# State-space slots: the output projection multiplies as plain fp32, without high and low parts

## The reference, cut to what matters

```python
proj = xn @ in_proj_w.T
z, xc, B, C, dt = jnp.split(proj, [...], axis=-1)
...                                    # convolution, silu, scan over time -> ys
y = jnp.moveaxis(ys, 0, 1).reshape(b, s, D_INNER)
y = _rms(y, inner_norm_w)              # divides by one root mean square per token, times a weight
y = y * jax.nn.silu(z)
out = y @ out_proj_w.T                 # 3072 -> 256
return x + out * RES_MULT
```

## Time and profile before

| | us |
|---|---|
| time, median of 3 runs (3034.8 to 3040.43) | 3035.02 |
| span of the profiled execution | 3067.1 |
| of it, state-space stage, from about | 1517 |
| PE / DVE / ACT / POOL busy over the span | 2711.5 / 2384.6 / 2110.9 / 1973.4 |

### The profile page before, as it was taken

One profiled execution on the slowest core, in us unless ns is written; L12 is line 12 of the kernel. 1 busy time (PEld: TensorE's weight loads), 2 busy tenths in 40 slices (PEclk: granted clock), 3 DMA queues, 4 the chain that ended last, 5 costly groups with the idle time before them and its releaser, 6 DMA issues.

```text
span 3067.1 us, 58582 instructions
## 1 busy us (share of the span) xinstructions
PE 2711.5 (88%) x17318; PEld 2120.1 (69%) x17318; DVE 2384.6 (78%) x5972; ACT 2110.9 (69%) x4670; POOL 1973.4 (64%) x1697
## 2 busy tenths in 40 slices
PE   4799999998569888379799999999999999999997
PEld 2466666665469765267588788787887878878786
DVE  3466666666377589558599999998899999999896
ACT  4444454443255466346599999998999999999996
POOL 3322222214424214555399999998999999999998
PEclk7799999997889899689899999999999999999999
DMA  6355445455766544446777776767666666676673
GB/s 168 94 176 170 168 165 185 149 195 168 238 178 199 168 154 151 157 128 199 230 240 237 236 237 205 220 204 220 219 206 217 205 210 216 205 224 199 203 218 113
DMA packets 320436, 588.35 MB, mean 192 GB/s; under 512 B 47888, under 2 KB 138800, under 8 KB 319632
## 3 DMA queue, kind: packets, MB, share of 16 engines
q1 hardware_dynamic: 305776, 545.07, 57.6%
q0 software_dynamic: 14352, 39.54, 3.5%
HBM read 464.44 MB, written 124.17 MB: 192 GB/s over the span
## 4 chain that ended last, share of the span: by engine, by line
POOL 34%; issue 10%; ACT 3%; DVE 1%; PE 1%; DMA 1%; POOLq 1%; SPq 0%; ACTq 0%; DVEq 0%
POOL mm L2706 8%; POOL y L2719 7%; POOL yz L2723 7%; POOL y L2733 6%; POOL y_lo L2712 6%; ACT mt L2636 1%; DVE cv L2789 1%; DMA wi<-ssm_wi_split 1%; POOLq L2382 1%; ACT ys L2650 0%; ACT mt L2656 0%; DVE bank L2860 0%; ACT L2671 0%; POOL first L2748 0%; PE bank L64 0%
## 5 line engine op out<-in xcount | busy, mean ns | idle before, releaser
L2706 POOL TENSOR_TENSOR mm<-mt,cb 128x512 f32<-128x512 f32 x384 | 490.2, 1299 | 56.9 <-ACT mt L2656 54.9
L2636 ACT ACTIVATE mt<-a_wide,a_tok 128x128 f32<-128x128 f32 x1536 | 487.1, 389 | 3.5 <-POOL mm L2706 2.5
L2789 DVE SCALAR_TENSOR_TENSOR cv<-bank,taps,cv 128x509 f32<-128x509 f32 (+2 forms) x576 | 429.3, 745 | 13.6
L64 PE MATMUL bank<-f,wi 128*128 128x512 f32 x768 | 322.4, 420 | 14.7 <-DMA wi<-ssm_wi_split 14.6
L65 PE MATMUL bank<-f,wi 128*128 128x512 f32 x768 | 305.7, 398 | 0.0
L66 PE MATMUL bank<-f,wi 128*128 128x512 f32 x768 | 305.7, 398 | 0.0
L2723 POOL TENSOR_TENSOR yz<-y,zs 128x512 f32<-128x512 f32 x192 | 249.2, 1298 | 15.0
L2712 POOL TENSOR_TENSOR y_lo<-yz,y_hi 128x512 fp32r<-128x512 f32 x192 | 246.2, 1282 | 8.4 <-ACT y_hi L2661 6.5
L2719 POOL TENSOR_TENSOR y<-t 128x512 f32<-128x512 f32 x192 | 246.0, 1281 | 0.0
L2529 PE MATMUL bank<-mm,x_tok 128*64 128x128 f32 x3072 | 226.4, 283 | 13.1 <-POOL mm L2706 13.1
L2733 POOL TENSOR_TENSOR y<-y,ys 128x512 f32<-128x512 f32 x184 | 237.6, 1292 | 0.1
(11 more groups left out here) (476 smaller groups left out, 8067.5 us busy)
## 6 DMA issues: line engine op xcount, KB each, us to landing
wi<-ssm_wi_split SPq DMA_DIRECT2D x192, 512.0 KB
a_wide<-a_scratch SPq DMA_DIRECT2D x192, 512.0 KB
l_fw<-ffn_split SPq DMA_DIRECT2D x72, 768.0 KB
ea<-ea_scratch SPq DMA_DIRECT2D x384, 128.0 KB
wo<-ssm_wo_split SPq DMA_DIRECT2D x192, 256.0 KB, 4.1
sorted_scratch<-ex_zeros SPq DMA_DIRECT2D x96, 130.5 KB
ssm_wi_split<-l_s_out SPq DMA_DIRECT2D x24, 512.0 KB
ey_x<-sorted_scratch SPq DMA_DIRECT2D x94, 130.5 KB
```

Source lines behind the costliest of these rows:

```text
L64: pe.matmul(out, wh, xh, start=first, stop=False)
L2636: i = act.activation(mt[:, h, chunk(j)], a_wide[:, g % R, h, chunk(j)], ACT.Relu, bias=a_tok[:, s * NJ + j, 2 * t + h:2 * t + h + 1], scal ...
L2706: pl.tensor_tensor(mm[:, :, ts], mt[:, :, ts], cb[:, js, :].rearrange("p j t -> p (j t)") .unsqueeze(1).broadcast_to([P, 2, TS // 2]), ALU ...
L2789: dve.scalar_tensor_tensor(cv[:, a:TS], bank[:, X, 0:TS - a], taps[:, t, k:k + 1], cv[:, a:TS], ALU.mult, ALU.add).then_inc(ph["tap"], 1)
```

## The change

The out-projection weights are no longer split. In the first stage GpSimd computes the low half only for the 512 in_proj columns of a state-space tile, ScalarE makes its copy in two instructions (512 and 256 columns, the second as plain fp32), and the scratch for them holds 256 columns instead of 512. In `ssm`, `output_high` and `output_low` are gone, `project_out` reads `yz` and `wo` directly with one plain fp32 matmul per bank, and `yz` is released by `out` instead of `y_lo`.

```diff
@@ ScalarE, first stage
-                    if n >= NT:
-                        done(act, "s_wo", n - NT)
-                    act.activation(s_out[:, 0:MLP], s_raw[:, 0:MLP], ACT.Copy).then_inc(ph["high"], 1)
+                    if n < NT:
+                        act.activation(s_out[:, 0:MLP], s_raw[:, 0:MLP], ACT.Copy).then_inc(ph["high"], 1)
+                        return
+                    act.activation(s_out[:, 0:MP_IN], s_raw[:, 0:MP_IN], ACT.Copy)
+                    done(act, "s_wo", n - NT)
+                    act.activation(s_out[:, MP_IN:MLP].bitcast(F32), s_raw[:, MP_IN:MLP], ACT.Copy).then_inc(ph["high"], 1)
@@ GpSimd, first stage
-                    pl.tensor_tensor(s_out[:, MLP:2 * MLP], s_raw[:, 0:MLP], s_out[:, 0:MLP].bitcast(F32), ALU.subtract).then_inc(ph["low"], 1)
+                    w = MLP if n < NT else MP_IN
+                    pl.tensor_tensor(s_out[:, MLP:MLP + w], s_raw[:, 0:w], s_out[:, 0:w].bitcast(F32), ALU.subtract).then_inc(ph["low"], 1)
@@ ssm
-        wo = sb("wo", [P, R, 2 * MP_OUT], F32R)
+        wo = sb("wo", [P, R, MP_OUT])
-        y_hi, y_lo = sb("y_hi", [P, TS], F32R), sb("y_lo", [P, TS], F32R)
@@ TensorE, project_out
-                    done(pe, "y_lo", g)
+                    done(pe, "yz", g)
                     landed(pe, "wo", g)
                     if t == 0:
                         done(pe, "evac", s - 1)
                     for m in range(KD):
-                        a = m * P
-                        i = mm3(pe, bank[:, OUT + m, :], (wo[:, g % R, a:a + P], wo[:, g % R, MP_OUT + a:MP_OUT + a + P]),
-                                (y_hi[:], y_lo[:]), t == 0, t == LAST)
+                        i = pe.matmul(bank[:, OUT + m, :], wo[:, g % R, m * P:(m + 1) * P], yz[:, g % 2], start=t == 0, stop=t == LAST)
@@ ScalarE: output_high and its call in beat k (item k-4) are gone
-                    act.activation(y_hi[:], yz[:, g % 2], ACT.Copy).then_inc(ph["y_hi"], 1)
@@ GpSimd: output_low and its call in beat k (item k-4) are gone
-                    pl.tensor_tensor(y_lo[:], yz[:, g % 2], y_hi[:].bitcast(F32), ALU.subtract).then_inc(ph["y_lo"], 1)
@@ GpSimd, outputs
-                    done(pl, "y_lo", g - 2)
+                    done(pl, "out", g - 2)
                     pl.tensor_tensor(yz[:, g % 2], y[:], zs[:, g % NS], ALU.mult).then_inc(ph["yz"], 1)
```

More of the change, by code:

```diff
@@ L129, in program @@
         wi_dram = nc.dram_tensor("ssm_wi_split", (NCT, P, 2 * MP_IN), F32, kind="Internal").ap()
-        wo_dram = nc.dram_tensor("ssm_wo_split", (NCT, P, 2 * MP_OUT), F32, kind="Internal").ap()
+        wo_dram = nc.dram_tensor("ssm_wo_scaled", (NCT, P, MP_OUT), F32, kind="Internal").ap()
         a_drams = (a_dram, nc.dram_tensor("a_scratch1", (HM, T), F32, kind="Internal").ap())
@@ L428, in keep @@
                     else:
-                        parts = s_out[:].bitcast(F32).rearrange("p (h c) -> p h c", h=2)
-                        sp.dma_start(wi_dram[n - NT].rearrange("p (h c) -> p h c", h=2), parts[:, :, 0:MP_IN]).then_inc(ph["s_kept"], 16)
-                        sp.dma_start(wo_dram[n - NT].rearrange("p (h c) -> p h c", h=2), parts[:, :, MP_IN:MLP]).then_inc(ph["s_kept"], 16)
+                        parts = s_out[:].bitcast(F32)
+                        sp.dma_start(wi_dram[n - NT].rearrange("p (h c) -> p h c", h=2),
+                                     parts.rearrange("p (h c) -> p h c", h=2)[:, :, 0:MP_IN]).then_inc(ph["s_kept"], 16)
+                        sp.dma_start(wo_dram[n - NT], parts[:, MP_IN:MLP]).then_inc(ph["s_kept"], 16)
                 def clear(a):
@@ L2430, in weights_out @@
                     done(sp, "out", g - R)
-                    sp.dma_start(wo[:, g % R, :].bitcast(F32), wo_dram[g % NCT]).then_inc(ph[f"wo{g % R}"], 16)
+                    sp.dma_start(wo[:, g % R, :], wo_dram[g % NCT]).then_inc(ph[f"wo{g % R}"], 16)
                 def inputs(s):
@@ L2656, in decays @@
                         act.activation(mt[:, :, ts], mt[:, :, ts], ACT.Exp, scale=-1.0).then_inc(ph["ex"], 1)
-                def output_high(g):
-                    done(act, "yz", g)
-                    done(act, "out", g - 1)
-                    act.activation(y_hi[:], yz[:, g % 2], ACT.Copy).then_inc(ph["y_hi"], 1)
                 def tokens(g):
@@ L2680, in _ @@
                         convolve(k)
-                    if has(k - 4):
-                        output_high(k - 4)
                     if has(k):
@@ L2707, in decayed @@
                                          .unsqueeze(1).broadcast_to([P, 2, TS // 2]), ALU.mult).then_inc(ph["mm"], 1)
-                def output_low(g):
-                    done(pl, "y_hi", g)
-                    done(pl, "out", g - 1)
-                    pl.tensor_tensor(y_lo[:], yz[:, g % 2], y_hi[:].bitcast(F32), ALU.subtract).then_inc(ph["y_lo"], 1)
                 def outputs(g):
@@ L2765, in _ @@
                         decayed(k - 1)
-                    if has(k - 4):
-                        output_low(k - 4)
                     if has(k - 3):
```

## The result

The changed kernel takes 3054.59 us (median of 4 runs, 3054.1 to 3058.65), the kernel before 3036.2 in the same comparison. The ratio is 1.0061, 95% interval [1.0046, 1.0075]: **slower by 18.4 us, 0.6%**. The forecast was 3069, or +34, with a range of 3048 to 3090.

A forecast was written before the change was run, and what follows sets the result against it. The prediction took TensorE (PE) to bound the ordinary beat. Its terms, +8.2, +24.6, +4.1, -2.0 and -1, with 0 for the first stage, came to +34 us: 3035 + 34 = 3069, range 3048 to 3090.

The forecast's parts named there:

- That TensorE bounds the ordinary beat: State-space stage: TensorE's own work is 7.64 us a beat, becoming 7.96 (early beats 7.86, becoming 8.18); chance 0.72.
- what GpSimd gives back: Ordinary beats: removing `y_lo` (1.28 us) returns no more than GpSimd's lag behind TensorE, 0.03 to 0.16 us a beat.
- +0.32 a beat: Output projection on TensorE: six products (1.40 us) give way to four fp32 passes (1.72 us), taken as 0.316.
- The first load: Rival, output projection: the first weight load is exposed each time, +0.10 in 190 beats, +19 us, 3088; chance 0.13.
- Slots: State-space stage, 24 beats each: cost 7.6 us, give back 2.3 + 1.2, so +4.1 each; six make +24.6.
- the stall: One beat 5.7 us too long on a late weight DMA: TensorE arriving later may take up some, -1, up to -5.
- The end of the program: After the last beats: some 2.5 us won on GpSimd's chain, limited by the last projection at the lower clock, -2.0.
- The rule on the weight loads' share: Weight loads busy 82% would mean TensorE has 18% left and GpSimd, at 99%, is the bound.
- the first rival: Ordinary beats: GpSimd is the bound and TensorE has room, -0.65 x 168 = -109 us, 2926 or so; chance 0.07.
- Two of the signs: Changed profile: GpSimd busy about 83% and waiting for ScalarE's `mt`; the chain of waits moved from GpSimd to PE.
- the first stage: GpSimd's subtraction shrinks (15 us) without gain; 24 more small ScalarE instructions, some 5 us; counted 0, with -3 to +4.
- the slots' ends: Three beats there run 4.4 us over TensorE's own work, of which about 1.2 go; giving back more favours 3048.

The follow-up runs named there:

- TensorE's part alone: The kernel before with only TensorE's output product changed to one plain fp32 matmul per bank, weights' low part left out; `y_hi` and `y_lo` still made: 3073.99 us, ratio 1.0123.
- GpSimd's alone: The kernel before without GpSimd's `y_lo` subtraction, TensorE multiplying `y_hi` in its place, six products as before: 3015.96 us, ratio 0.9933.
- the runs with the copies alone: The kernel before with one edit, ScalarE copying a first-stage state-space tile in two instructions (512, then 256 columns after the scaling wait): 3026.74 us, ratio 0.9965.
- the run with one copy: The changed kernel with ScalarE's first-stage copy put back to one instruction of 768 columns after the scaling wait: 3066.75 us, ratio 1.0103.
- the version with two products: The kernel before with ScalarE's two copies and two products per bank, fp32r `yz` by the weights' high and low parts, y's low part dropped: 2977.51 us, ratio 0.9804.

## Why the prediction was right, and where it was off

- **That TensorE bounds the ordinary beat** and that what GpSimd gives back is at most 0.03 to 0.16 a beat, is shown from both sides. TensorE's part alone costs 37, GpSimd's alone gains 21, where its 246.2 us of busy time and the chain promised ten times that.
- **+0.32 a beat for four passes at 0.43 against six products at 0.233**: measured 1.72 for the four, and 7.95 where 7.96 was forecast (8.18 in the early beats, as forecast). The first load was not exposed in the ordinary beats: the record of the four is 1.88 long and not 1.98.
- **Slots**: the forecast was 194.2 between two `mean_square`, +4.1; 24 beats of the changed kernel take 194.2. The stage from first to last scores pass was forecast 36.9 longer, before the stall, and is 35.9 in the profiled pair.
- **The end of the program**: -2.0 forecast, -3.8 in the profiled pair (-0.5 in the run where `y_hi` and `y_lo` stayed). The beat with the late weight DMA gave nothing clear: the 24 beats around it went from 195.4 to 199.4, where the forecast had PE take up 1 us; in the other experiments with the plain product they took 196.1 to 200.2.
- **The rule on the weight loads' share**, which the prediction cites from the Trainium skill, would have led to the first rival. With PEld at 82% TensorE had no room, and GpSimd's removal alone gave 21 us, not 109. Here the measurement decides against reading that share as headroom.
- **Two of the signs** were off. GpSimd is busy 80% of the ordinary beats (36.87 of 46.00), not 83%, and it waits for `ys` as well as for `mt`. And the move of the chain to PE cannot be read: on the changed kernel's page no line of the chain has 1% of the span.
- **The term that was mis-sized is the first stage**: I counted 0 with -3 to +4; it is about -11 by the runs with the copies alone, -12 by the run with one copy, and -14 to -16 by the starts of the state-space stage. The step looked only at what the two edited instructions cost, ScalarE's at +5 and GpSimd's at -15 that it could not use. It did not see that the `done(act, "s_wo", ...)` moved behind two thirds of the copy, nor did it ask what the granted clock would do there. The wait that the move shortens was in the profile before the change (73.5 us in front of line 796, under the view by line), and the forecast had quoted GpSimd's 205.3 us of waiting for exactly that instruction without asking what ScalarE itself was waiting for. With -11 to -14 there the sum would have been +20 to +23.
- The forecast difference was nearly twice the measured one. It was wrong in one place, outside the stage that the change is about, and the total fell inside the range partly by luck: the range reached down to 3048 for the stall and the slots' ends, with no more than 3 us for the first stage. The run with one copy, 3066.75, is the forecast without that place.
- The 32 us between the span before and the median lay almost all ahead of the stage (1523.5 against 1491.5 to 1493.4), so carrying only the difference over was right.

## What to carry to other kernels

When all engines are over 90% busy, read the pace of each from starts: find one beat in which the suspect waits for nothing, and one in which it waits. Here an instruction removed from the engine that the chain names bought no more than its lead over the next engine, and what that next engine got on top was paid in full. And when an edit moves a wait behind part of the work, look up what that wait costs today, even in a stage that the change only touches in passing.

## What the runs showed of the hardware

- A plain fp32 matmul of 512 columns took two passes of 0.43 us, 0.86 in all, at the full granted clock (1.00, the 2.4 GHz level); an fp32r product took 0.233. Three fp32r products (0.70) were cheaper on TensorE than one plain fp32 matmul. Between other plain fp32 matmuls and the transposes the passes followed without extra time.
- In the program's last microseconds TensorE waited 3.02 us for GpSimd's squares, and from 3043.0 to 3046.6 its granted clock was 0.55 on average, near the 1.2 GHz level. Four such passes are 3.37 us long there by record (1.88 at the full clock), which puts the last scaling behind TensorE instead of behind ScalarE:

```profile
3043.23 3.37 PE L2568 MATMUL bank<-yz,wo 128*128 128x512 f32 x4
...
3046.64 1.23 DVE L2848 TENSOR_TENSOR bank<-bank,yr 128x1024 f32<-128x1024 f32 x1 [10.16 <-PE bank L2568]
```

- VectorE's busy share understated how full it was: 44.42 of 46 us in the version with two products, while its instructions followed one another with no wait. What lies in between, 0.26 a beat, are gaps of 0.04 to 0.07 us from one instruction to the next.

```profile
2000.00:2046.00 46.00, 45.55 (x321) 36.63 (x320) 44.42 (x108) 40.47 (x101) 39.21 (x31) 1.00 0.67 222
```
